# The last RMS norm of a transformer layer: its rstd applied to tokens as they leave PSUM, its gain folded into the router, gate and up weights

## The reference

```python
h = layernorm(x) * (1 + ca) + sa
x = x + ga * attn1(h)                      # 16 heads of 8, relative position bias
h = layernorm(x) * (1 + cb) + sb
x = x + gb * ffn(h)

def ffn(x):
    h = x + attn2(rmsnorm(x, g1))          # rotary, causal
    return h + moe(rmsnorm(h, g2))
def rmsnorm(x, w): return x * rsqrt(mean(x * x) + eps) * w
def moe(x):
    probs = softmax(x @ w_router); top 2 of 8 experts, weights normalised to sum 1
    out = sum over the two: topw * (silu(x @ wg[e]) * (x @ wu[e])) @ wd[e]     # hidden 384
```

## Time and profile before

| | us |
|---|---|
| median of 3 runs | 1074.74 (1070.42 to 1076.9) |
| profiled execution, device time | 1070.41 |
| its span in the trace, first to last instruction | 1068.3 |
| PE / DVE / ACT / POOL busy in the span | 907.6 / 698.0 / 529.0 / 227.1 |
| granted TensorE clock, mean | 0.935 of full speed |

### The profile page before, as it was taken

One profiled execution on the slowest core, in us unless ns is written; L12 is line 12 of the kernel. 1 busy time (PEld: TensorE's weight loads), 2 busy tenths in 40 slices (PEclk: granted clock), 3 DMA queues, 4 the chain that ended last, 5 costly groups with the idle time before them and its releaser, 6 DMA issues.

```text
span 1068.3 us, 36323 instructions
## 1 busy us (share of the span) xinstructions
PE 907.6 (85%) x15358; PEld 560.1 (52%) x15358; DVE 698.0 (65%) x1534; ACT 529.0 (50%) x908; POOL 227.1 (21%) x274
## 2 busy tenths in 40 slices
PE   6776878988899998898899699989899777887893
PEld 3343434545455554455444345555456466776792
DVE  2465576576769785957765777786657665556573
ACT  2424535456374755355555166556354343445452
POOL 1520020000102102022110200021222245443352
PEclk9889999699999999999998699999898999999896
DMA  7395800000000000000000100000000012226423
GB/s 202 165 312 182 313 22 8 2 7 3 27 17 13 27 13 12 7 23 17 17 13 15 27 13 13 3 17 18 12 25 24 27 55 61 61 57 180 121 62 118
DMA packets 50045, 61.74 MB, mean 58 GB/s; under 512 B 5600, under 2 KB 36064, under 8 KB 49504
## 3 DMA queue, kind: packets, MB, share of 16 engines
q1 hardware_dynamic: 34624, 28.03, 9.0%
q10 hardware_dynamic: 10272, 21.14, 5.8%
q0 software_dynamic: 4992, 10.27, 3.0%
HBM read 23.76 MB, written 35.65 MB: 56 GB/s over the span
## 4 chain that ended last, share of the span: by engine, by line
PE 46%; DVE 24%; issue 13%; ACT 8%; POOL 4%; another core or an unknown queue 3%; DMA 2%; POOLq 0%; SPq 0%; DVEq 0%; ACTq 0%
DVE row_max L1188 14%; PE ps L838 8%; PE ps L689 5%; PE ps L722 5%; PE ps L734 4%; PE ps L923 3%; PE ps L670 3%; POOL eo_rows L1477 3%; PE ps L700 2%; PE ps L664 2%; ACT stage L963 2%; ACT k_head L963 2%; PE ps L728 1%; PE ps L915 1%
## 5 line engine op out<-in xcount | busy, mean ns | idle before, releaser
L1188 DVE TENSOR_REDUCE row_max<-ps 128x4 f32<-128x1024 f32 (+1 forms) x256 | 266.1, 1079 | 57.0 <-PE ps L700 30.6
L1025 ACT ACTIVATE probs<-ps 128x1024 f32<-128x1024 f32 x128 | 130.0, 1027 | 104.5 <-PE ps L722 89.1
L1025 ACT ACTIVATE stage<-ps 128x1024 f32<-128x1024 f32 x96 | 98.0, 1024 | 88.8 <-PE ps L728 79.9
L689 PE MATMUL ps<-bias_t,ch 64*32 64x512 f16 x2048 | 112.2, 408 | 26.9 <-DVE row_max L1188 18.1
L1477 POOL DMA_INDIRECT eo_rows<-eo_t,to_t x92 | 88.8, 965 | 117.7 <-ACT eo_t L1075 98.6
L1432 POOL TENSOR_TENSOR rstd_n<-var_n,cf 128x2 f32<-128x2 f32 x48 | 34.4, 717 | 370.8 <-DVE var_n L1125 370.6
L915 PE MATMUL ps<-xT_t,wgu_hi 128*128 128x256 f16 x276 | 77.2, 280 | 21.3 <-DVE hid L1360 12.5
L1355 DVE SCALAR_TENSOR_TENSOR gate_s<-gate_t,ps 128x256 f32<-128x256 f32 x138 | 57.4, 416 | 48.1 <-ACT gate_t L1069 41.8
L1464 POOL DMA_INDIRECT slot_rows<-rows,slots x64 | 64.0, 1000 | 107.2 <-DVE slots L1304 92.9
L838 PE MATMUL ps<-probs,v_pad 128*32 128x256 f32 x1024 | 84.9, 399 | 1.9 <-issue 1.2
L1069 ACT ACTIVATE gate_t<-ps 128x256 f32<-128x256 f32 x138 | 52.5, 383 | 63.3 <-PE ps L917 42.3
(11 more groups left out here) (169 smaller groups left out, 1697.4 us busy)
## 6 DMA issues: line engine op xcount, KB each, us to landing
slot_rows<-eo_g ACTq DMA_DIRECT2D x1, 12642.0 KB, 41.0
slot_rows<-eo_g ACTq DMA_DIRECT2D x1, 7998.0 KB, 26.1
x_t<-slot_rows SPq DMA_DIRECT2D x46, 129.0 KB
eo_g<-eo_rows SPq DMA_DIRECT2D x16, 256.0 KB, 3.3
xT<-in_x SPq DMA_DIRECT2D x16, 128.0 KB, 2.0
kept<-resid SPq DMA_DIRECT2D x16, 128.0 KB, 1.7
resid_b<-kept SPq DMA_DIRECT2D x16, 128.0 KB
out_dram<-outT SPq DMA_DIRECT2D x16, 128.0 KB
```

The lines of the kernel that those rows point to most:

```text
L689: eng.matmul(ps[HR * c:HR * (c + 1), lo + r, :].rearrange("p (j s) -> p j s", j=2), csth("flip")[half, :], bias_t[half, way, 2 * g:2 * g + ...
L1025: eng.activation(probs[a][:, 2 * (k % 2):2 * (k % 2) + 2, :], ps[:, lo:lo + 2, :], ACT.Exp).then_inc(z["exp"], 1)
L1188: ins = eng.tensor_reduce(row_max[a][:, qt, 4 * g:4 * g + 4].rearrange("p (r j) -> p r j", r=2), of_heads, AX.X, ALU.max)
```

## The change

`spread.r2` and `n.r2` are gone, and `r2T` with them. `tok` works on `h2T` itself and doesn't wait for the norm. The factor has tokens on partitions, as the transposed tokens in PSUM have, so ACT applies it as its per-partition scale while copying (two instructions of 128x256 in place of one of 128x512), DVE in the subtraction (two `scalar_tensor_tensor` in place of one `tensor_tensor`) and in the copy of the logits (two in place of one). The gain `g2` is multiplied once into the router matrix and into `wgu`, on ACT (`act_gains`: 128x8, and twice 128x3072), before POOL splits the matrices. `root.r2` writes one of two buffers by item.

```diff
     def b2(self, i):
-        last = self.chain("b2", i, last, ("sq.r2", "act", 0.42), ("var.r2", "pe", 0.45, SHARED), ("v.r2", "dve", 0.16, (), "mine"),
-                          ("root.r2", "pool", 0.72))
-        last = self.op(("b2", i, "spread.r2"), "pe", 0.45, [last] + ([("h", i - 1, "tok")] if i else []), SHARED)
-        last = self.op(("b2", i, "n.r2"), "dve", 0.48, [last], (), "mine")
+        last = self.chain("b2", i, last, ("sq.r2", "act", 0.42), ("var.r2", "pe", 0.33, SHARED), ("v.r2", "dve", 0.16, (), "mine"))
+        last = self.op(("b2", i, "root.r2"), "pool", 0.72, [last] + ([("h", i - 2, "top")] if i > 1 else []))
     def h(self, i):
-        last = self.op(("h", i, "tok"), "pe", 0.8, [("b2", i, "end")] + self.before("h", i), SHARED)
-        last = self.op(("h", i, "rows"), "act", 0.40, [last] + ([("h", i - 2, "end")] if i > 1 else []))
-        last = self.op(("h", i, "top"), "dve", 1.9, [last], (), "mine")
+        last = self.op(("h", i, "tok"), "pe", 0.8, [("b2", i, "h2")] + self.before("h", i), SHARED)
+        last = self.op(("h", i, "rows"), "act", 0.75, [last, ("b2", i, "end")] + ([("h", i - 2, "end")] if i > 1 else []))
+        last = self.op(("h", i, "top"), "dve", 2.4, [last], (), "mine")
     def weights(self):
-        last = ("f1", 0, "root.n1")
+        last = self.op(("w", 0, "gain0"), "act", 2.7, [("f1", 0, "root.n1"), ("w", 0, "load")])
+        self.op(("w", 0, "gain1"), "act", 2.7, [last])
         for n, us in enumerate((2.8, 6.0, 2.8, 6.0, 1.5)):
-            last = self.op(("w", 0, n), "pool", us, [last, ("w", 0, "load")])
+            last = self.op(("w", 0, n), "pool", us, [last] + ([("w", 0, "gain1")] if n == 2 else []))
         def pe_h(eng, i):
-            eng.wait_ge(norm["r2"]["n"], i + 1)
+            if i == 0:
+                eng.wait_ge(su["routed"], 1)
+            eng.wait_ge(h2_done, i + 1)
             for t in range(KT):
-                eng.transpose(flat[:, t * P:(t + 1) * P], r2T[:, t * P:(t + 1) * P], ident)
+                eng.transpose(flat[:, t * P:(t + 1) * P], h2T[:, t * P:(t + 1) * P], ident)
+        def act_gains(eng):
+            yield PLACE["w", 0, "gain0"]
+            eng.wait_ge(s_w2, 16 * N_W2)
+            eng.activation(wr[:, :], wr[:, :], ACT.Copy, scale=gains[:, 1:2]).then_inc(su["routed"], 1)
+            eng.wait_ge(s_moew, 32)
+            for k in range(2):
+                if k:
+                    yield PLACE["w", 0, "gain1"]
+                eng.activation(wgu[:, k, :], wgu[:, k, :], ACT.Copy, scale=gains[:, 1:2]).then_inc(su["routed"], 1)
         def act_h(eng, i):
-            eng.activation(rows[:, i % 2, :, :, 0:D], tokens_twice(i), ACT.Copy).then_inc(hand["hi"], 1)
+            eng.wait_ge(norm["r2"]["root"], i + 1)
+            for t in range(KT):
+                ins = eng.activation(rows[:, i % 2, :, t, 0:D], tokens_twice(i, t), ACT.Copy, scale=rstd_r2[:, i % 2, t:t + 1])
+            ins.then_inc(hand["hi"], 1)
         def dve_h(eng, i):
-            eng.tensor_tensor(rows[:, i % 2, :, :, D:2 * D], tokens_twice(i), rows[:, i % 2, :, :, 0:D], ALU.subtract) \
-               .then_inc(hand["lo"], 1)
+            eng.wait_ge(norm["r2"]["root"], i + 1)
+            for t in range(KT):
+                ins = eng.scalar_tensor_tensor(out=rows[:, i % 2, :, t, D:2 * D], in0=tokens_twice(i, t),
+                                               scalar=rstd_r2[:, i % 2, t:t + 1], in1=rows[:, i % 2, :, t, 0:D],
+                                               op0=ALU.mult, op1=ALU.subtract)
+            ins.then_inc(hand["lo"], 1)
-            eng.tensor_copy(logit[:, :, :], held("h", i, "tok")[:, S:S + KT * NX].rearrange("p (t x) -> p t x", t=KT)) \
-               .then_inc(hand["l"], 1)
+            for t in range(KT):
+                ins = eng.tensor_scalar(logit[:, t, :], held("h", i, "tok")[:, S + t * NX:S + (t + 1) * NX],
+                                        rstd_r2[:, i % 2, t:t + 1], None, ALU.mult)
+            ins.then_inc(hand["l"], 1)
         def pool_moe_weights(eng):
             for k in range(2):
                 yield PLACE["w", 0, 2 * k]
-                eng.wait_ge(s_moew, 32)
+                eng.wait_ge(su["routed"], k + 2)
         def pool_norm(eng, pre, i, at):
+            if pre == "r2" and i > 1:
+                eng.wait_ge(hand["lo"], i - 1)
+                eng.wait_ge(hand["l"], i - 1)
```

More of the change, by code:

```diff
@@ L562, in block_kernel @@
         su = signals("su_", "filled casts offsets by silu mod modcopy "
-                            "gate wsplit v2filled")
-        norm = {n: signals(n + "_", "sq var v root spread n" + (" h" if n[0] == "n" else "")) for n in ("n1", "n2", "r1", "r2")}
+                            "gate routed wsplit v2filled")
+        norm = {n: signals(n + "_", "sq var v root" + ("" if n == "r2" else " spread n") + (" h" if n[0] == "n" else "")) for n in ("n1", "n2", "r1", "r2")}
         att = {a: signals("a%d_" % a, "mean xc qk v hi vz lo kspread qspread krow qrow score max "
@@ L635, in held, with tokens_twice @@
             return ps[:, BANK_OF[key], :]
-        def tokens_twice(i):
-            tok = held("h", i, "tok")[:, 0:S].rearrange("p (t d) -> p t d", t=KT)
-            return tok.unsqueeze(1).to_broadcast([P, 2, KT, D])
+        def tokens_twice(i, t):
+            return held("h", i, "tok")[:, t * P:(t + 1) * P].unsqueeze(1).to_broadcast([P, 2, D])
         def pe_setup(eng):
@@ L665, in pe_norm @@
             ins.then_inc(z["var"], 1)
+        def pe_norm(eng, pre, job, i, at):
+            z = norm[pre]
+            yield from pe_var(eng, pre, job, i, at)
             yield at("spread." + pre)
@@ L859, in pe_b2 @@
             yield from pe_back(eng, 2, i, at)
-            yield from pe_norm(eng, "r2", "b2", i, at)
+            yield from pe_var(eng, "r2", "b2", i, at)
         def pe_h(eng, i):
@@ L1119, in dve_mod, with dve_var @@
             eng.wait_ge(su["gate"], 8)
+        def dve_var(eng, pre, job, eps, i, at):
+            yield at("v." + pre)
+            eng.wait_ge(norm[pre]["var"], i + 1)
+            eng.tensor_scalar(var[pre][:, :], held(job, i, "var." + pre)[:, 0:KT], eps, None, ALU.add).then_inc(norm[pre]["v"], 1)
         def dve_norm(eng, pre, job, eps, src, mult, dst, shift, i, at):
             z = norm[pre]
-            yield at("v." + pre)
-            eng.wait_ge(z["var"], i + 1)
-            eng.tensor_scalar(var[pre][:, :], held(job, i, "var." + pre)[:, 0:KT], eps, None, ALU.add).then_inc(z["v"], 1)
+            yield from dve_var(eng, pre, job, eps, i, at)
             yield at("n." + pre)
@@ L1247, in dve_b2 @@
             eng.wait_ge(h2_done, i + 1)
-            yield from dve_norm(eng, "r2", "b2", RMS_EPS, h2T[:, :], gains[:, 1:2], r2T[:, :], None, i, at)
+            yield from dve_var(eng, "r2", "b2", RMS_EPS, i, at)
         def dve_h(eng, i):
```

10 lines of the change are left out of this document (5 added, 5 removed).

## The result

The changed kernel takes 1107.91 us (median of 4 runs, 1105.01 to 1110.22), the kernel before 1072.97 us on the same chip: a ratio of 1.0314, with an interval of 1.0274 to 1.0354. The forecast was 1073.0 with a range up to 1087. It is wrong by 35 us, on the slow side.

The account below looks back on a forecast made before the run. PE, busy 85% and most often on the chain, was taken to set the pace, with no engine full. The terms -9.2 + 2.1 + 5.4 = -1.7 us gave 1073.0 us at the median, own range 1066 to 1080, with rivals 1060 to 1087.

Parts of the forecast that it names:

- The removal: Attention hand-overs: dropping spread.r2 (8.3 us on the chain) and n.r2 (0.85) removes 9.2 us, lower bound 4.6.
- Rival (B): PE's gap is filled by nothing, the freed slot becomes a wait and only costs stay: 1082 us; chance 0.17.
- The hand-over: ACT copies, DVE subtractions and logits copies split in two, on the chain for 5, 10, 10 items: +2.1 us.
- The gains: At the start, ACT scales wr and wgu among item 0's exponentials, near 47 us: +5.4 us, bounds 0 and 8.
- POOL stays hidden, with 4 us to spare: At the start, POOL's later split ends near 69 us, before PE's first f2 step at 73.
- The order: All engines' order is planned anew: 6 us either way allowed, about the spread of the three runs.
- The sum: Whole kernel: -9.2 + 2.1 + 5.4 = -1.7 us, giving 1068.7 against the profiled execution, 1073.0 at the median.
- (A): Idle waits, such as DVE's before n.r2, go as well: 1062 us with half, 1053 with all; chance 0.19.
- (C): tok takes a shared PSUM bank early and holds it up to 19.9 us an item: 1087 us; chance 0.18.
- The 10 expert tiles: Attention stage: nine expert tiles ran there before 864 us; each one moved out by the new order costs 4.4 us.

Follow-up runs that it names:

- removal_only: Kernel before, same order, without spread.r2 and n.r2; single unscaled copies kept, factor and g2 left out of what follows: ratio 1.0003.
- late_split: Kernel before with POOL's split of wgu held until the eighth exponential of item 0, no gains on ACT: ratio 1.0073.
- old_order: All instructions of the change, every engine in the order of the kernel before, gains behind item 0's sixth and eighth exponentials: ratio 1.0167.
- gains_alone: Kernel before plus ACT scaling wr and wgu behind item 0's sixth and eighth exponentials, POOL's split waiting for it: ratio 1.0100.
- dve_gains: Changed kernel with g2 multiplied in by DVE, in its gap behind qk_lo of item 1, instead of by ACT: ratio 1.0126.
- after: The changed kernel itself, against the kernel before on the first chip: 1107.91 us, ratio 1.0314.
- early_gains: Changed kernel with both gains ahead of item 0's first exponential and the transposes planned behind the factor: ratio 1.0021.
- early_gains_again: Repeat of early_gains, unaltered, against the kernel before on a quick chip (1028.5 us): ratio 1.0054.

## Why the prediction was wrong, point by point

**The removal, -9.2 us.** Failed. "I take the full 8.3 + 0.85 = 9.2 us as removed": measured 0 (`removal_only`, 1.0003 with an interval of -0.3 to +0.3%), outside the lower bound of 4.6 too. Twelve of sixteen spreads on the chain did not mean that twelve gaps close. (The chain has thirteen, with 9.1 us: the one near 813 us stands in one piece with another norm's spread, 1.54 us at 811.93. That makes the miss larger.) Rival (B) was right here, and its argument against itself ("twelve of sixteen spreads were on it") was the weak one.

**The hand-over, +2.1 us.** Mis-sized: 4 to 5 us (1.0047 against 1.0003 in the same order; the intervals just overlap). The pieces: I took 0.38 us for ACT's 128x256 copies and 0.416 for DVE's, and they take 0.475 and 0.475; the logits' copies take 0.219 each in place of 0.166 for the one. As pairs they take 0.84 us where the one took 0.60, 0.87 where it took 0.69, and 0.35 where it took 0.17; with my counts of 5, 10 and 10 items that makes about 5 us, an estimate that fits. The rows I went by were near in size but had constants as scalars, or none. The Trainium skill has the difference for ACT: "ScalarE: Activation LUTs", section "What ACT_TABLE_LOAD costs", says that each per-partition pointer operand adds about 93 ns. The trace agrees: a copy of this size with a constant scale took 0.383 us before (L1069), the new one takes 0.475. For DVE, L1355, which I took as the same form, has a constant where the new instruction has a factor from a tile.

**The gains, +5.4 us.** Place, length and path were right: 48.76 and 53.31 us where I said 47 and a little later, 2.88 us where I said 2.7, the first `f2` step 6.4 us later (74.3) where I said 5, through ACT, for which PE waited 5.00 us. "POOL stays hidden, with 4 us to spare" held for PE, with 3.3 (71.0 against 74.3). It did not hold for DVE, whose product stood 1.8 us longer behind POOL's subtraction; PE waited 0.16 us for that in the changed kernel, and 2.2 to 5.9 us in `late_split`, `old_order`, `gains_alone` and `dve_gains`. The price was wrong: 10 us by `gains_alone`, 10.5 on the slow chip, 6 and 13 in other orders. The step that failed is that a wait of PE costs its own length. PE was busy 1.00 of 6 us, the clock loss ahead of the first `h2T` rose by 10 us, and the first `h2T` moved by 9.4. The sum has no term for it. That the wait caused the lower clock behind it is argued, not shown.

**The order, +-6 us.** Too narrow for the slow chips: +14.6 us there, the largest single term; on the quick ones between -2 and +7, within the bound. A planner that gets a shorter estimate for one step moves the time by 0.4% with no work changed. Why the planned order costs so much on a slow chip stays open.

**The sum.** -9.2 + 2.1 + 5.4 = -1.7 was the forecast. By the runs of the slow chip it is 4.4 + 10.5 + 14.6 = 29.5 us, with the removal's 0 inside the 4.4. This is no test of the parts: each is the step from one kernel to the next, so they must add up to the 1.0273. All four terms erred to the same side, and none had the clock in it: by the medians of these runs the clock loss grew by 26 us and the rest by 3. As the time rises by 0.7 us for each us of clock loss among the executions of the kernel before on this chip, some 18 of the 29 us go with the clock, an estimate.

**Rivals.** (A) did not come: no idle time was saved. (B) was right in kind for the removal; its 1082 lacks the clock and the order. (C) did not come: from `tok` to the subtraction a mean of 3.4 us passes, 6.6 at most, where 2.2 was the mean before and 8 my bound. By its own price that is about 1 us. Planning the transposes late gives back 0.3 to 0.7%, with overlapping intervals; whether that is the place of the transposes or the new order is not separated. A slower result for other reasons is not a point for it. The 10 expert tiles ahead of the last `h2T` (9 before) also went as said, since none was lost.

## What to carry to other kernels

A piece of the chain is an offer, not a saving: before counting it, look at what PE does with a freed place, for here, with PE busy 86%, less work left the time as it was, with more waiting and a slightly lower clock. A collision that one variant shows need not be what another pays for: look at what PE waits for in the changed kernel itself. Before moving work in time, list what every neighbour runs in the new place, above all DVE instructions with two SBUF inputs beside POOL instructions that read SBUF, and put work that must be added into idle time that the trace already shows (late gains cost 6 to 13 us here; put early, they and the longer hand-over together cost 4). When an order is planned anew, run the old work in a new order once, to know how much of a difference the order makes by itself.

## What the runs showed of the hardware that was not expected

- DVE's product with two SBUF inputs, 0.67 us alone, took 2.47 (`after`), 3.20 (`late_split`), 5.86 (`gains_alone`) and 6.47 us (`dve_gains`) beside a running POOL subtraction of 6.0 us, and ended some 0.5 us behind it.
- The granted clock may follow small changes. `removal_only` gave PE 64 matmuls less and the median clock fell from 0.941 to 0.937, just outside the scatter; in the changed kernel the clock stood at 0.50 to 0.59 in stretches from the gap of PE on. That the gap is the cause is argued from their order in time, and not shown.
- One program, two executions (`early_gains`, `early_gains_again`): level at the first `f2` step, 2.5 us apart at the first `h2T`, with 12.3 and 4.0 us of clock loss between.
- The same program takes 1028 to 1031 us on three chips and 1073 to 1081 on two. On the slow ones PE falls behind at 13 places of one program and 15 of the other, 1 to 5 us each, in part standing still and in part at the lower clock; for the changed kernel the two slow chips show them at the same instructions.
- A scale or factor from a tile makes ACT's 128x256 copy out of PSUM 0.475 us and DVE's 0.475.
